# The maximum loads of both attention layers issued by ScalarE instead of SyncE

## The reference, cut to what matters

```python
q, k, v = proj(layernorm(x)), proj(ctx), proj(ctx)      # 16 heads of 8
scores = q @ k.T / sqrt(8)                              # + mask * -1e9 in layer 1
x = x + softmax(scores) @ v @ Wo + bo
```

## Time and profile before

| | |
|---|---|
| median of 3 executions | 570.29 us |
| the profiled execution | 571.93 us, span 570.1 us |
| TensorE matmuls busy | 479.2 us (84%) |
| VectorE busy | 351.3 us (62%) |
| ScalarE busy | 310.1 us (54%) |
| GpSimd busy | 202.1 us (35%) |
| attention layer 0, bodies with exponentials | about 53 to 193 us |
| feed-forward block | about 193 to 265 us |
| attention layer 1, bodies with exponentials | about 294 to 460 us |
| experts | about 460 to 557 us |

### The profile page before, as it was taken

One profiled execution on the slowest core, in us unless ns is written; L12 is line 12 of the kernel. 1 busy time (PEld: TensorE's weight loads), 2 busy tenths in 40 slices (PEclk: granted clock), 3 DMA queues, 4 the chain that ended last, 5 costly groups with the idle time before them and its releaser, 6 DMA issues.

```text
span 570.1 us, 12397 instructions
## 1 busy us (share of the span) xinstructions
PE 479.2 (84%) x3906; PEld 397.3 (70%) x3906; DVE 351.3 (62%) x1258; ACT 310.1 (54%) x675; POOL 202.1 (35%) x431
## 2 busy tenths in 40 slices
PE   2448999999998899974889999999999898499980
PEld 1237677777766589963777877777777678499970
DVE  8885777778774156756577778678778433112203
ACT  2213676767767525563476666565666654246540
POOL 7240002231222223445110012543543657765550
PEclk9998999999999999996799999999999999889995
DMA  6404333243322990004454324334320120232107
GB/s 167 118 29 132 101 114 96 89 132 98 90 65 107 422 371 28 3 1 142 127 178 128 100 76 127 99 106 121 115 72 18 47 52 20 79 84 74 44 19 221
DMA packets 52267, 60.06 MB, mean 105 GB/s; under 512 B 7633, under 2 KB 43354, under 8 KB 50928
## 3 DMA queue, kind: packets, MB, share of 16 engines
q1 hardware_dynamic: 47248, 52.99, 29.7%
q0 software_dynamic: 2272, 4.24, 2.3%
q10 hardware_dynamic: 2688, 2.10, 1.2%
HBM read 30.01 MB, written 29.23 MB: 104 GB/s over the span
## 4 chain that ended last, share of the span: by engine, by line
PE 49%; DVE 5%; issue 4%; ACT 4%; DMA 4%; POOL 3%; SPq 1%; POOLq 0%; ACTq 0%; DVEq 0%
PE ps L1493 6%; PE ps L1546 6%; PE ps L1734 5%; PE ps L1724 5%; PE ps L1529 5%; PE ps L1549 5%; PE ps L1458 3%; PE ps L1460 2%; PE ps L1459 2%; ACT probs L906 2%; PE ps L1558 1%; DMA k_dram<-qk_parts 1%; DMA k_blocks<-y_dram 1%; PE ps L1785 1%; PE ps L1702 1%
## 5 line engine op out<-in xcount | busy, mean ns | idle before, releaser
L906 ACT ACTIVATE probs<-ps 128x512 f32<-128x512 f32 x256 | 147.6, 597 | 77.2 <-PE ps L1549 72.4
L1529 PE MATMUL ps<-k_blocks,q_stacks 128*128 128x256 f32 x512 | 119.8, 318 | 15.0 <-DVE row_max L1145 8.1
L1153 DVE CUSTOM_DVE_ANT_0 ps<-ps,mask_q 128x256 f32<-128x256 f32 x256 | 102.7, 452 | 38.4 <-PE ps L1529 37.5
L1549 PE MATMUL ps<-q_stacks,k_blocks 128*128 128x256 f32 x512 | 105.9, 291 | 1.7 <-DMA q_stacks<-maxT 1.6
L1145 DVE TENSOR_REDUCE row_max<-ps 128x2 f32<-128x512 f32 x128 | 84.2, 687 | 30.8 <-PE ps L1529 29.7
L1549 PEld LDWEIGHTS ps<-q_stacks,k_blocks 128*128 128x128 f32 x512 | 87.3, 190 | 21.6 <-issue 10.6
L1529 PEld LDWEIGHTS ps<-k_blocks,q_stacks 128*128 128x128 f32 x512 | 81.6, 198 | 21.5 <-DVE row_max L1145 10.8
L1493 PE MATMUL ps<-probs,v_aug 128*32 128x256 f32 x1024 | 68.5, 385 | 4.8 <-ACT probs L906 3.7
L765 POOL TENSOR_SCALAR max_split<-row_max 128x16 fp32r<-128x16 f32 x32 | 6.5, 204 | 180.7 <-DVE row_max L1145 81.3
L1546 PE MATMUL ps<-mask_k,neg_mask_eye 128*128 128x512 f32 x128 | 54.5, 426 | 0.2 <-DMA q_stacks<-maxT 0.2
L710 POOL DMA_INDIRECT y_dram<-x_ring x39 | 41.2, 1058 | 24.5 <-ACT x_ring L1004 18.5
(11 more groups left out here) (212 smaller groups left out, 821.0 us busy)
## 6 DMA issues: line engine op xcount, KB each, us to landing
slots_dram<-x_ring SPq DMA_DIRECT2D x1, 10400.0 KB, 28.8
q_stacks<-q_dram SPq DMA_DIRECT2D x32, 256.0 KB
q_dram<-qk_parts SPq DMA_DIRECT2D x16, 384.0 KB, 3.6
k_dram<-qk_parts SPq DMA_DIRECT2D x16, 384.0 KB, 3.9
k_blocks<-k_dram SPq DMA_DIRECT2D x128, 48.0 KB
x_ring<-slots_dram SPq DMA_DIRECT2D x39, 65.0 KB, 2.0
ctx_in<-ctx SPq DMA_DIRECT2D x16, 128.0 KB, 2.2
mask_in<-mask_Bx1xSxS_ik SPq DMA_DIRECT2D x8, 256.0 KB, 2.9
```

The lines of the kernel that those rows point to most:

```text
L906: eng.activation(probs[:, n // HPS % 2, n % HPS, :, :].rearrange("p k q -> p (k q)"), ps[:, head_bank(BANKS_T, n)[0], :], ACT.Exp).then_in ...
L1153: last = eng.tensor_tensor_reduce(out=scored, in0=scored, in1=mask_q[1 - r][:, i, :], scale=1.0, scalar=-3.0e38, op0=ALU.add, op1=ALU.max, ...
L1529: mm = eng.matmul(ps[:, bank, i * S:(i + 1) * S], q_stack[r][:, st, i * P:(i + 1) * P], k_blocks[r][:, st, j, :], start=True, stop=True)
L1549: mm = eng.matmul(ps[:, bank, k * S:(k + 1) * S], k_blocks[r][:, st, j, k * P:(k + 1) * P], q_stack[r][:, st, :], start=(l == 0), stop=(l ...
```

## The change

Both calls of `max_loads` leave SyncE's body. `max_copy` calls it at its end, so ScalarE waits for its own copy and then issues the two DMAs on its own queue; 64 DMAs move, 32 for each layer. In body 0 of each layer SyncE gets a wait in their place, for the first copy of the maxima, ahead of its `stack_loads` of half 1. Nothing else is edited.

```diff
                 if exists(b + 1):
                     if exists(b - 1):
                         eng.wait_ge(a.t_ps, b * 16)
+                    elif exists(b):
+                        eng.wait_ge(a.mT_sb, 1)
                     stack_loads(eng, a, b + 1, 1 - r, 1)
-                if exists(b):
-                    max_loads(eng, a, b, r, 1)
                 if exists(b + 2):
                     eng.wait_ge(a.qk_lo, b + 3)
...
                     stack_loads(eng, a, b + 2, r, 0)
-                if exists(b + 1):
-                    max_loads(eng, a, b + 1, 1 - r, 0)
...
                     if n == at["a_max1"] and exists(b):
-                        max_copy(b, 1)
+                        max_copy(b, r, 1)
...
                     if n == at["a_max0"] and exists(b + 1):
-                        max_copy(b + 1, 0)
+                        max_copy(b + 1, 1 - r, 0)
...
-            def max_copy(b, half):
+            def max_copy(b, r, half):
                 eng.wait_ge(a.mT_ps, b * 2 + half + 1)
...
                 eng.activation(maxT[:, half, :, :].rearrange("p s q -> p (s q)"), ps[0:2 * HPS, bank, :],
                                ACT.Copy).then_inc(a.mT_sb, 1)
+                max_loads(eng, a, b, r, half)
```

## The result

The changed kernel takes 586.72 us in the median of four runs (585.66 to 588.19) against 570.54 us before: 16.2 us between the medians. The ratio of the runs is 1.0265, 95% interval 1.0229 to 1.0300, or 15.1 us. In a second session it was 588.80 against 572.75, ratio 1.0279 (1.0230 to 1.0328). The prediction had the sign and the mechanism; at 578.4 us it had half of the size, and the measured median lies 0.7 us above its range. The profiled execution after took 585.66 us, with a span of 583.9.

What follows compares the result with a forecast made beforehand. TensorE was taken to set the attention layers' pace. Terms 2.8 + 1.4 + 0.7 - 0.5 + 1.5 + 0.6 + 1.0 + 0.65 = 8.15 us on the 570.29 us median gave 578.4 us, range 571 to 586.

Steps and rivals of the forecast that it cites:

- The stall: ScalarE after each maximum copy: two issues take 1.08 us, plus 0.04; the next exponential is 1.21 us late.
- Layer 0, half 0: Behind step 11: TensorE's head 14 is late, 0.4 us in each of seven bodies, 2.8 us, bounds 0 and 5.2.
- Half 1: Layer 0, behind step 0: 0.2 us for each of bodies 0 to 6, 1.4 us; last body 0.7 us.
- Start of layer 0: First maxima of layer 0: TensorE's 0.54 us wait at 53.31 goes, no exponential displaced, -0.5 us.
- Layer 1: Half 0 free; half 1 costs 0.6 us over six bodies, 1.0 in body 0, 0.65 in the last.
- what SyncE does earlier: End of layer 0: the `slots_dram` fill runs beside the last half 0 load, 1.5 us, bounds 0 and 3.2.
- held behind SyncE: Rival, layer 0's last two copies: ScalarE's issue waits for SyncE's stuck issue, up to 10.7 us; 585 us, chance 0.12.
- A long issue near 180 us: Sign of a wrong forecast: one long ScalarE issue near 175 or 180 us makes most of the loss.
- The stall is covered: Rival, decided at layer 0's head 14: exponentials catch up before TensorE needs them; 568.7 us, chance 0.05.

Runs made afterwards that it cites:

- half 1 only: ScalarE issues only the half 1 loads, the `slots_dram` fill held behind the last maxima, against the kernel before: 579.95 us, ratio 1.0107.
- layer 1 only: ScalarE issues the maximum loads in layer 1 only, layer 0 as in the kernel before: 574.73 against 571.31 us, ratio 1.0087.
- the last batch alone: Only the two loads of layer 0's last batch move to ScalarE, against the kernel before: 579.10 against 572.09 us, ratio 1.0124.

## Why the prediction was half right

**The stall** came as worked out. The pair of issues takes 1.05 us for 1.08, the next exponential starts 0.1 to 0.2 us behind it instead of 0.04, and head 14 waits 0.50 us, for 0.47 forecast.

**Layer 0, half 0:** 0.53 us a body for 0.4, but in six bodies instead of seven, so about 3 us for 2.8: the sum of the term came out by luck of two errors. I had let the 0.15 us wait at head 0 absorb some; that the late shifted products also delay the scores of head 15, the maxima of VectorE and their split would explain the rest, and was not tried alone. **Half 1:** 0.23 to 0.3 us a body for 0.2, and 0.73 us in the last body for 0.7. **Start of layer 0:** priced at -0.5, measured at nothing that can be told; the wait for the stack loads is there with or without the maxima.

**Layer 1:** 2.8 us for 2.25. Body 0 (1.06 for 1.0) and the last body (0.60 for 0.65) came in the places and at the sizes named. The 0.1 us a body between them, 0.6 us in all, did not: bodies 2 to 5 are free, body 1 lost 0.52 us and body 6 0.63. In body 6, without projections for a further batch, TensorE reaches the weighted product sooner and waits 0.62 us for its exponentials; why body 1 loses stays open.

**The step that failed is the term "what SyncE does earlier"**, 1.5 us with bounds 0 and 3.2, measured at 7. The mechanism was named: the advanced fill beside the last half 0. Three things were missing. The bound came from the 5.4 us landing of one context load, read as one in the same crowd; but that load was issued at 210.50 us, when the fill (180.62 + 28.8) had landed. Landing 8 KB in the midst of the fill took 5.1 us from the end of the issue, 3.8 more than before. The issue itself doubled, which stopped ScalarE 2.2 us and TensorE 1.5. And the two waits took TensorE's clock to 0.50 for some 6 us; no part of the sum had a price for what follows a wait. With 7 in place of 1.5 the sum gives 8.15 + 5.5 = 13.7 us, and with the other terms as measured (half 0 at 3, half 1 at 1.6 to 2.1, the start at 0, layer 1 at 2.8) it gives 15.1 to 15.6, against 15.1 by the ratio and 16.2 by the medians.

**The rival "held behind SyncE"** forecast 585 us, close to the measured time, for the wrong reason: with SyncE silent the issues were as long. A long issue near 180 us, named as a sign that the forecast is wrong, did come, but it was 2.11 us and not up to 10.7, and held no more than 1.5 us of TensorE's time. The Trainium skill (DMA: Bandwidth & Descriptors, section Queues, rings and completion order) says that each DMA engine takes turns between the queues packet by packet, so a queue of one's own spares an 8 KB load the 10.4 MB ahead of it, but not its turns; 5.1 us of landing instead of 1.3 agrees with that. What makes the issue itself longer no run here shows beyond that it comes with the traffic.

**"The stall is covered"** decided at 0.70 us between the copy and head 14, and there the point held: one issue of 0.51 us fits (b3h1 to b7h0 as before), two don't.

## What to carry to other kernels

A DMA issue on a computing engine costs only what is needed soon behind it: find, in the timeline, the instruction behind the issue and the moment at which another engine needs it, and put the issue where the engine waits anyway, one instruction later if that lets it run beside the work ahead. Before taking a wait out of a queue, look at what stands behind it: here it had kept 10.4 MB of traffic away from two 8 KB loads that the critical path needed, and that was nearly half the loss. A wait of several microseconds on TensorE must be priced with the clock that follows it.

## What the runs showed of the hardware

- Issue time grows with traffic: of the 32 pairs in the kernel after, 29 took 1.04 to 1.08 us to issue, and the two of batch 7 took 2.11 and 1.83 us in the midst of a 10.4 MB store from another queue, with that other queue silent as well as stuck. 0.4 us after the start of the store it was still 1.06.
- The first pair of `max_loads` that ScalarE issues took 1.65 or 1.66 us in nine kernels: at 48 to 50 us in most, at 55.30 with half 1 only and at 288.76 with layer 1 only, so it is not the place that makes it long; what does, no run shows. In the kernel with the last batch alone the first pair falls into the store (2.17 us), so the growth with traffic rests on the kernels where it doesn't.
- The sequencer issues beside a running activation (121.00 to 122.07, with an exponential from 120.88 to 121.45), if it has no wait for that activation; an activation behind the issue starts 0.1 us after its end.
- After 1.5 and 3.4 us of waiting within some 6 us, TensorE ran at 0.50 of its clock from 186 to 192 us, and the same 16 products took 1.94 us instead of 1.07.
